# Attention and filter kernel: the seams between its stages laid over each other, with constant multiplies on PE in one wait

## The chip, the cores and the metric

The kernel runs as one program on one core of one Trainium2 chip. The metric is the device time of one execution in microseconds (us). A core has five engines with instruction streams of their own, which are ordered against each other by semaphores alone: PE (TensorE, matrix multiplies), DVE (VectorE), ACT (ScalarE), POOL (GpSimd) and SP (SyncE, which here issues every DMA). PE's clock has two levels, 1.2 and 2.4 GHz; the profile gives it as a share of the full one.

## The reference, cut to what matters

The input is x with shape (8, 512, 128, 128) in float32. Two layers are added to it in turn, each behind a group normalisation over 16 channels:

```python
def _gn(v, G=32, eps=1e-5):
    g = v.reshape(B_, G, C_ // G, H_, W_)
    m = jnp.mean(g, axis=(2, 3, 4), keepdims=True)
    s = jnp.var(g, axis=(2, 3, 4), keepdims=True)
    return ((g - m) / jnp.sqrt(s + eps)).reshape(v.shape)

# layer 0: 8 heads of 64 channels, S = H * W positions
A = jnp.einsum('mi,bhis->bhms', Wa, xh) + ba[:, None]
Bm = jnp.einsum('ni,bhis->bhns', Wb, xh) + bb[:, None]
V = jnp.einsum('ni,bhis->bhns', Wv, xh) + bv[:, None]
attn_maps = jax.nn.softmax(Bm, axis=-1)
attn_vecs = jax.nn.softmax(V, axis=2)
G = jnp.einsum('bhms,bhns->bhmn', A, attn_maps)
Z = jnp.einsum('bhmn,bhns->bhms', G, attn_vecs)

# layer 1: 12-tap separable filters; up by 2, bias, leaky, clip, down by 2
y = _upfirdn2d_sep(x, up_filter, UP, 1, PADDING, float(UP * UP))
y = y + bias[None, :, None, None]
y = jnp.where(y >= 0, y, y * SLOPE) * GAIN
y = jnp.clip(y, -CLAMP, CLAMP)
y = _upfirdn2d_sep(y, down_filter, 1, DOWN, (0, 0, 0, 0), 1.0)

x = x + layer0(_gn(x)); x = x + layer1(_gn(x))
```

## The kernel before, in words

The work is cut into 32 units of 128 channels of one image (two heads, eight normalisation groups). One pass of a loop, written out for each engine, does one unit. x is held twice: `xc` with channels on the partitions, `xh` with image rows on the partitions.

1. **Scores** (L1049 on PE, `max_b` L770 on DVE, `exp_b` on ACT, `gather_h` L439 on POOL): 32 blocks of four columns. ACT gathers a block of xc into `xcb`, a ring of four that lies in `yb` (L147), and PE projects it. DVE keeps a running maximum, ACT takes the exponential, PE transposes it, DVE copies that, and PE multiplies it with a block of xh that POOL has gathered into `xn`. POOL's gather waits until all of the unit's xh is loaded.
2. **Values** (L1087 on PE, `max_v` L818 on DVE): 32 blocks. Each block is projected twice, its maximum spread by POOL and subtracted by PE, the exponential taken and multiplied (`z`); DVE normalises it, POOL adds it to xh (L447).
3. **Norm 1, group 0** (L834 to L848): DVE takes the statistics of 16 channels of xh, PE averages them over the partitions (L1102), and the scales follow. Then batches 0 and 1 are normalised (L885, L891), in a high and a low float16 part (`xn_2`).
4. **Filters** (L1185 on PE, L604 on ACT, L928 on DVE, L484 on POOL): 16 batches g of eight images. In step i of batch g, PE makes the up-rows of image i of batch g+1 (`up_rows`, into bank 6), the up-columns of image i of g and the down-rows of image i-2. ACT evicts the up-rows (`t1` high) and the up-columns (`yb`), DVE makes the low part of t1 (L898) and the leaky step (L943), POOL clips (L458). In step 0, PE also makes the remainder rows from `t1r`, which POOL copies out of t1 (L487) as the first thing of a batch, after the clip of the batch before. Batch g+2 is normalised by ACT (L588, L592), and POOL makes its low part (L482). The statistics of group 1 are taken in step 0 of batch 0 (`group_stats`, L832).
5. **Tail** (L1220 on PE): what is left of batch 15, and between it norm 0 for the next unit: DVE's statistics and scales (L718 to L742), an average and a product on PE (L1006, L1010), a square root on ACT. The next unit's scores start when all of it is done.

The order on each engine is written out by hand. `steps` (L272) unrolls the first and last passes of a stage and loops over the ones between. `then_inc` raises a semaphore when an instruction ends, `wait_ge` holds the engine. On PE, the tail and the head of the unit are

```python
                for half in range(2):
                    down_remainder(half, last_ps[half])
...
                pe.wait_ge(s_y, IMG * NBAT * u + YCREDIT)
                pe.wait_ge(s_w, u + 1)
                proj_b(0, 0)
                proj_b(1, 1)
                pe.wait_ge(s_o, 2 * NBAT * u + OCREDIT)
                steps(pe, NBLK, RING, attend)
```

with the loop's jump between them.

## Time and profile before

| | |
|---|---|
| runs, us | 16610.16, 16631.77, 16636.97; median 16631.77 |
| profiled execution, us | 16617.44 (span 16615.7) |
| instructions in the span | 487793 |
| granted PE clock, mean | 0.96 |
| busy share of PE, DVE, ACT, POOL | 88%, 75%, 68%, 54% |
| DMA, mean | 72 GB/s |
| chain that ended last, by engine | PE 59%, DVE 14%, issue 8%, ACT 8%, POOL 5%, DMA 3% |
| DVE leaky step, 128x532 (L943), x4096 | mean 775 ns |
| POOL clip, 128x532 (L458), x4096 | mean 634 ns, idle before it 4108.1 us, ended by DVE L943 |
| PE, matmuls of the down rows (L987, dn_t with yb), x32768 | 4402.1 us busy |

The profile is that of one execution; its own time is 14 us under the median of the runs. The busy shares are means over stages that differ: in some stages PE has no gap, in others it mostly waits. "issue" is time in which an engine waited for nothing that the profile shows. All matmuls of a helper have one line (L987), so they are told apart by their tiles. Times in the trace are us from the start of the span. One unit takes 516.9 us (from 5226.7 to 5743.6 in the trace, the unit used below).

### The profile page before, as it was taken

Reading aid. Unit: us, or ns where it says so; the run is one execution under the profiler, and the core shown is the slowest. Engines: PE = TensorE matmul, PEld = TensorE weight load, DVE = VectorE, ACT = ScalarE, POOL = GpSimd, SP = SyncE. Lnnn points to the kernel's source line nnn. Section 1 sums busy time; section 2 is a strip of 40 time slices with the busy share of each in tenths; the row PEclk is TensorE's granted clock in tenths of the full one; section 3 lists DMA queues with packets and bytes.
Section 4 is the critical chain, followed back from the end, with each engine's and each line's share of the span. In section 5 each row is a group of like instructions: output and inputs, shape, how many; then the busy total and the mean of one; then the engine's idle time right before and its main releaser. Section 6 shows DMA issues by size and latency. Waiting matters only on the chain.

```text
span 16615.7 us, 487793 instructions
## 1 busy us (share of the span) xinstructions
PE 14628.5 (88%) x156388; PEld 12544.6 (75%) x156388; DVE 12382.1 (75%) x26154; ACT 11322.1 (68%) x19746; POOL 9035.6 (54%) x13589
## 2 busy tenths in 40 slices
PE   7898888988889888898888888888888889888898
PEld 5777777777777777777777777777777777777787
DVE  6777777777777777777777777777777777777776
ACT  5676666766667666676666666666667666676676
POOL 4555555555555555555555555555555555555555
PEclk9999999999999999999999999999999999999999
DMA  3233222332222332223322233222332223322232
GB/s 82 59 81 90 72 61 60 78 90 75 62 62 75 88 79 60 62 73 88 83 61 61 69 88 85 63 59 66 88 86 62 61 64 87 89 64 60 63 86 49
DMA packets 1931549, 1199.83 MB, mean 72 GB/s; under 512 B 78724, under 2 KB 1864580, under 8 KB 1930244
## 3 DMA queue, kind: packets, MB, share of 16 engines
q1 hardware_dynamic: 1930244, 1183.65, 27.6%
q8 instruction: 670, 10.98, 0.3%
q14 instruction: 635, 5.20, 0.1%
HBM read 537.30 MB, written 268.44 MB: 48 GB/s over the span
## 4 chain that ended last, share of the span: by engine, by line
PE 59%; DVE 14%; issue 8%; ACT 8%; POOL 5%; DMA 3%; DVEq 1%; POOLq 1%; SPq 1%; ACTq 0%
PE ps L987 57%; ACT yb L613 4%; DVE yb L943 4%; DVE xh L913 3%; POOL yb L458 3%; PE ps L1057 2%; ACT z L597 2%; DVE t L898 1%; DVE sth L832 1%; DMA out<-xh 1%; POOL t1r L487 1%; DVE z L904 1%; DVE stc L656 1%; DMA p<-t 1%; DMA xh<-in_x 1%
## 5 line engine op out<-in xcount | busy, mean ns | idle before, releaser
L458 POOL TENSOR_SCALAR yb<-yb 128x532 f32<-128x532 f32 x4096 | 2595.8, 634 | 4108.1 <-DVE yb L943 4108.1
L987 PE MATMUL ps<-dn_t,yb 128*128 128x64 f32 (+1 forms) x32768 | 4402.1, 278 | 10.5 <-POOL yb L458 10.5
L987 PEld LDWEIGHTS ps<-dn_t,yb 128*128 128x128 f32 x32768 | 4075.4, 196 | 19.7 <-POOL yb L458 14.4
L943 DVE SCALAR_TENSOR_TENSOR yb<-yb 128x532 f32<-128x532 f32 x4096 | 3174.6, 775 | 971.1 <-ACT yb L613 949.2
L613 ACT ACTIVATE yb<-ps,bias_b 128x532 f32<-128x532 f32 x4096 | 2881.2, 703 | 884.9 <-PE ps L987 794.9
L987 PE MATMUL ps<-up,xn 128*128 128x266 f16 x12288 | 2133.7, 287 | 640.0 <-DVE t L898 371.2
L585 ACT ACTIVATE t<-ps 128x266 f16<-128x266 f32 x4096 | 1587.6, 388 | 1534.5 <-PE ps L987 1482.0
L898 DVE TENSOR_TENSOR t<-ps,t 128x266 f16<-128x266 f32 x4096 | 1735.5, 426 | 801.2 <-ACT t L585 695.0
L987 PE MATMUL ps<-up_a,t 128*128 128x138 f16 x15360 | 2049.3, 225 | 11.2 <-DMA t<-p 11.0
L441 POOL COPY xn<-xh 128x512 f32 x1024 | 1090.6, 1067 | 1775.8 <-PE ps L987 1075.2
L987 PE MATMUL ps<-up_b,t 128*128 128x138 f16 x15360 | 2045.1, 224 | 0.0
L450 POOL TENSOR_TENSOR xh<-xh,pt 128x512 f32 (+1 forms) x1024 | 1692.0, 1652 | 524.2 <-DVE pt L815 521.1
L597 ACT ACTIVATE z<-ps 128x512 f16<-128x512 f32 x2048 | 1222.8, 597 | 721.3 <-PE ps L987 716.9
L987 PEld LDWEIGHTS ps<-up,xn 128*128 128x128 f16 x12288 | 1019.9, 103 | 872.9 <-DVE t L898 445.4
L904 DVE TENSOR_TENSOR z<-ps,z 128x512 f16<-128x512 f32 x2048 | 1405.4, 686 | 275.0 <-ACT z L597 205.9
L987 PEld LDWEIGHTS ps<-xn,pt 128*128 128x128 f32 x8192 | 1080.6, 194 | 559.0 <-issue 557.0
L987 PEld LDWEIGHTS ps<-gaug,p 128*128 128x128 f32 x8192 | 1070.1, 191 | 516.1 <-DVE pt L815 240.7
L987 PEld LDWEIGHTS ps<-up_a,t 128*128 128x128 f16 x15360 | 1347.2, 98 | 148.7 <-DMA t<-p 15.6
L482 POOL TENSOR_TENSOR xn<-xn 128x256 f16<-128x256 f32 x1792 | 1406.3, 805 | 0.0
L987 PEld LDWEIGHTS ps<-up_b,t 128*128 128x128 f16 x15360 | 1235.1, 98 | 0.0
L987 PE MATMUL ps<-yb,wbs 128*128 128x512 f32 x2048 | 1143.3, 649 | 99.8 <-ACT yb L533 95.8
L555 ACT ACTIVATE yb<-xc,sc 128x512 f32 (+1 forms) x1024 | 1198.5, 1170 | 0.0
(151 smaller groups left out, 27187.9 us busy)
## 6 DMA issues: line engine op xcount, KB each, us to landing
xc<-in_x SPq DMA_DIRECT2D x512, 512.0 KB, 3.8
xh<-in_x SPq DMA_DIRECT2D x480, 512.0 KB, 5.0
out<-xh SPq DMA_DIRECT2D x480, 512.0 KB, 3.4
p<-t SPq DMA_DIRECT2D x960, 128.0 KB, 3.0
t<-t SPq DMA_DIRECT2D x960, 128.0 KB, 2.4
t<-p SPq DMA_DIRECT2D x960, 128.0 KB, 2.4
xh<-in_x SPq DMA_DIRECT2D x64, 256.0 KB, 2.9
out<-xh SPq DMA_DIRECT2D x64, 256.0 KB, 3.0
```

What stands on the lines that cost most here:

```text
L441: nc.gpsimd.tensor_copy(xhb[par], xh_wc[:, bass.ts(k, WB), :]).then_inc(s_xhb, 1)
L450: nc.gpsimd.tensor_tensor(xv, xv, zs_[par][:].rearrange("p w h m -> p w (h m)"), ALU.add).then_inc(s_x1, 1)
L458: nc.gpsimd.tensor_scalar(v, v, CLAMP, -CLAMP, ALU.min, ALU.max).then_inc(s_yc, 1)
L482: return nc.gpsimd.tensor_tensor(xn_2[:, par, 1, c, :], xn[:, c, :], xn_2[:, par, 0, c, :], ALU.subtract)
L555: act.activation(xcb[r].rearrange("p (w h) -> p w h", w=WB), xc_wh[:, bass.ts(k, WB), :], ACT.Identity, bias=nm0).then_inc(s_xv, 1)
L585: act.activation(t1[:, par, 0, i, :], ps[:, bank, 0:UP], ACT.Copy).then_inc(s_th, 1)
L597: act.activation(z1[:, p // 2, 0, p % 2 * 2:p % 2 * 2 + 2, :, :].rearrange("p r c h -> p (r c h)"), dz_ps[p % 2], ACT.Copy).then_inc(s_zh, 1)
L613: act.activation(yb[:, i % YRING, :, :], y_ps[i % 2], ACT.Identity, scale=UPGAIN * GAIN, bias=bias_b[:, bass.ds(c0 + i, 1)]).then_inc(s_y, 1)
L898: nc.vector.tensor_tensor(t1[:, par, 1, i, :], ps[:, bank, 0:UP], t1[:, par, 0, i, :], ALU.subtract).then_inc(s_t1, 1)
L904: nc.vector.tensor_tensor(lo, dz_ps[p % 2], hi, ALU.subtract).then_inc(s_z1, 1)
L943: nc.vector.scalar_tensor_tensor(v, v, SLOPE, v, ALU.mult, ALU.max).then_inc(s_lr, 1)
L987: return nc.tensor.matmul(o, l, r, start=start, stop=stop, skip_group_check=share)
```

## The change

- **Scores of the next unit start in the tail.** `xcb` moves from yb into t1's half 0, free in the last batch. The last batch contains ACT's first four gathers, norm 0's steps on DVE, ACT and PE. In the tail the first four score blocks (`attend_first`, `exp_first`, `max_first`) stand between the last down rows and columns. The loop over score blocks starts at block 4. The tail's banks change (`last_ps`, `zr_ps`). The last unit is written out behind the loop on PE and ACT as well.
- **The last 16 channels of xh are loaded twice**: a copy for POOL's gather goes into xn_2 in the last batch (`load_copy`, 2 x 512 KB), and each gather becomes two copies.
- **Statistics of groups 0 and 1 under the values**: `block_stats`, two of 64 numbers per partition for each block.
- **PE multiplies constants** into bank 7: 42 times ahead of the wait for group 0's statistics and 26 times behind the average.
- **Batch 0 and 1**: normalisation in halves of four images; batch 1's on POOL (`first_batches`); in step 0 of batch 0, up-columns, eviction and leaky step come first.
- **All batches**: ACT's normalisation and POOL's low part in halves over four steps; `t1r` is copied ahead of the clip of image 7 of the batch before.

```diff
-        xcb = [yb[:, i, :, :].rearrange("p c u -> p (c u)")[:, 0:BS] for i in range(YRING)]
+        xcb_all = t1[:, 0, :, :, :].rearrange("p t i u -> p (t i u)").bitcast(fp32)
+        xcb = [xcb_all[:, i * BS:(i + 1) * BS] for i in range(RING)]
+        xlate = xn_2[:, :, :, :, :].rearrange("p a t i w -> p (a t i w)").bitcast(fp32).rearrange("p (c w) -> p c w", w=W)
+        xlate_wc = xlate.rearrange("p c w -> p w c")
...
+            def load_copy(u):
+                for i in range(0, LATE, IMG):
+                    sp.dma_start(xlate[:, i:i + IMG, :], x_row[u, :, P - LATE + i:P - LATE + i + IMG, :]).then_inc(s_xa, 16)
...
-                nc.gpsimd.tensor_copy(xhb[par], xh_wc[:, bass.ts(k, WB), :]).then_inc(s_xhb, 1)
+                nc.gpsimd.tensor_copy(xhb[par][:, :, 0:P - LATE], xh_wc[:, bass.ts(k, WB), 0:P - LATE])
+                nc.gpsimd.tensor_copy(xhb[par][:, :, P - LATE:P], xlate_wc[:, bass.ts(k, WB), :]).then_inc(s_xhb, 1)
...
+            def first_batches(u):
+                g = NBAT * u + 1
+                wait_alone(pool, s_r1, GROUPS * u + 1)
+                wait_alone(pool, s_xn, 2 * g)
+                for h in range(2):
+                    c = slice(h * HALF, (h + 1) * HALF)
+                    nc.gpsimd.tensor_scalar(xn[:, c, :], xh[:, IMG + h * HALF:IMG + (h + 1) * HALF, :], nm1[:, 0, 0:1],
+                                            r1[:, 0:1], ALU.add, ALU.mult).then_inc(s_xs, 1)
+                for h in range(2):
+                    norm_low_half(g, 1, h)
+                keep_rows(NBAT * u, 0)
...
             def clip_batch(u, j, par, before, after):
                 g = NBAT * u + j
-                wait_alone(pool, s_t1, IMG * (g + 1))
-                nc.gpsimd.tensor_copy(t1r[:, par, :, :, :], t1[:, par, :, :, 2 * P:UP].rearrange("p t i q -> p t q i")).then_inc(s_tq, 1)
                 for i in range(IMG):
+                    if i == IMG - 1 and after(1):
+                        keep_rows(g + 1, 1 - par)
                     clip_image(g, i, par)
                     if i == 1:
                         remainder_high(g, par)
                     if i == 2:
                         remainder_low(g, par)
                     now = 4 if before(1) else 6
-                    if after(2) and i in (now, now + 1):
-                        if i == now:
-                            wait_alone(pool, s_xnh, g + 3)
-                            wait_alone(pool, s_xs, g + 3)
-                        norm_low(par, 2 * (i - now))
-                        last = norm_low(par, 2 * (i - now) + 1)
-                        if i > now:
+                    if after(2) and i >= now:
+                        h, q = divmod(i - now, 2) if before(1) else (i - now, 0)
+                        if q == 0:
+                            wait_alone(pool, s_xnh, 2 * (g + 2) + h + 1)
+                            wait_alone(pool, s_xs, 2 * (g + 2) + h + 1)
+                        last = norm_low(par, 2 * h + q)
+                        if not before(1):
+                            last = norm_low(par, 2 * h + 1)
+                        if q or not before(1):
                             last.then_inc(s_xn, 1)
...
+                        now = 4 if first else LAG
+                        if i == now and after(2) and par == 0:
+                            act.wait_ge(s_r1, GROUPS * u + j // 2 + 2)
+                        if now <= i < now + 4 and after(2):
+                            if (i - now) % 2:
+                                xn_high(j + 2, par, 1, (i - now) // 2)
+                            else:
+                                norm(j + 2, 1, (i - now) // 2)
+                        if not after(1) and more:
+                            if i % 2:
+                                gather_first(u + 1, i // 2)
+                            if i == 4:
+                                sqrt0(u + 1)
...
+                if more:
+                    for k in range(RING):
+                        exp_first(u + 1, k)
...
+                def block_stats(k):
+                    for gr, st in enumerate((stc, stg)):
+                        last = nc.vector.bn_stats(st[:, bass.ds(k, 1), :].rearrange("p a b -> p (a b)"),
+                                                  xh[:, gr * GROUP:(gr + 1) * GROUP, bass.ts(k, WB)])
+                    return last
...
+                    if before(4):
+                        block_stats(k - 4)
...
-                        if first and i == 0:
-                            for p in range(4):
-                                last = group_stats(1, 1, p)
-                            last.then_inc(s_st1, 1)
...
+                        if more and not after(1):
+                            tail = base + N_SMALL - N_NORM0
+                            if i == 2:
+                                norm0_stats(u + 1, tail)
+                            if i == 4:
+                                norm0_variance(u + 1, tail)
+                            if i == 6:
+                                norm0_scales(u + 1, tail)
...
+                if more:
+                    max_first(u + 1, 0)
+                down_low(g, 3)
+                remainder_low(g, zr_ps)
+                if more:
+                    max_first(u + 1, 1)
                 for half in range(2):
-                    add_out(NBAT * (u + 1) - 1, NBAT - 1, half, last_ps[half])
+                    add_out(g, NBAT - 1, half, last_ps[half])
+                if more:
+                    for k in range(2, RING):
+                        max_first(u + 1, k)
...
+            def keep_busy(n):
+                for _ in range(n):
+                    mm(ps[:, 7, 0:UP], up_2[:, 0, 0:P], up_2[:, 0, :], True)
...
+                keep_busy(42)
                 pe.wait_ge(s_gn1, GROUPS * u + 1)
                 mm(tiny[:, 0:2], avg_p[:], mvh[:, 0, :], True).then_inc(s_gn1p, 1)
+                keep_busy(26)
...
+                        if not after(1) and more:
+                            if i == 3:
+                                norm0_average(u + 1)
+                            if i == 5:
+                                norm0_bias(u + 1)
...
                 steps(pe, NBAT, 2, batch, 2)
                 g = NBAT * (u + 1) - 1
+                if more:
+                    pe.wait_ge(s_w, u + 2)
+                    pe.wait_ge(s_y, IMG * (g + 1) - 1 + YCREDIT)
+                    proj_b(u + 1, 0, 0)
                 pe.wait_ge(s_z1, 4 * g + 2 + DCREDIT)
                 pe.wait_ge(s_o, 2 * g + OCREDIT)
                 down_columns(0, last_ps[0])
-                for i in range(IMG - LAG, IMG):
-                    if i == IMG - 1:
-                        norm0_average(u + 1)
-                    down_rows(g, i, 1)
+                down_rows(g, IMG - 2, 1)
+                if more:
+                    proj_b(u + 1, 1, 1)
+                down_rows(g, IMG - 1, 1)
                 pe.wait_ge(s_y, IMG * (g + 1) + YCREDIT)
+                pe.wait_ge(s_z1, 4 * g + 3 + DCREDIT)
                 remainder_columns(g, 1, zr_ps)
-                norm0_bias(u + 1)
+                if more:
+                    attend_first(u + 1, 0)
                 pe.wait_ge(s_z1, 4 * g + 4 + DCREDIT)
                 down_columns(1, last_ps[1])
                 pe.wait_ge(s_zr, g + 1 + ONE)
                 for half in range(2):
                     down_remainder(half, last_ps[half])
+                if more:
+                    pe.wait_ge(s_o, 2 * g + 1 + OCREDIT)
+                    attend_first(u + 1, 1)
+                    attend_first(u + 1, 2)
+                    pe.wait_ge(s_o, 2 * g + 2 + OCREDIT)
+                    attend_first(u + 1, 3)
```

POOL, steps 6 and 7 of a batch in the loop over batches, and the start of the next. L482 and L501 make the low part of xn, L487 and L512 the copy t1r, L458 and L477 the clip. Before:

```order
L482 TENSOR_TENSOR xn<-xn 128x256 x2
L269 REGISTER_ALU
L458 TENSOR_SCALAR yb<-yb 128x532
L269 REGISTER_ALU
L458 TENSOR_SCALAR yb<-yb 128x532
L461 COPY yc<-yb 128x2x20
L277 UNCONDITIONAL_BRANCH
L277 ISA
L487 COPY t1r<-t 128x160
L269 ISA
L458 TENSOR_SCALAR yb<-yb 128x532
```

With the change:

```order
L477 TENSOR_SCALAR yb<-yb 128x532
L275 REGISTER_ALU
L501 TENSOR_TENSOR xn<-xn 128x256
L275 REGISTER_ALU
L512 COPY t1r<-t 128x160
L275 REGISTER_ALU
L477 TENSOR_SCALAR yb<-yb 128x532
L480 COPY yc<-yb 128x2x20
L501 TENSOR_TENSOR xn<-xn 128x256
L283 UNCONDITIONAL_BRANCH
L283 ISA
```

The copy t1r stood behind the last clip and the jump of the loop; it stands ahead of the clip of image 7 now, and a quarter of the low part stands in each step.

PE, the end of a unit and the start of the next. wbs is the scaled weight of the scores, p0 and p1 the exponentials, xn the gathered block of xh. Before:

```order
L987 MATMUL ps<-dr_2,zr 128x4x5 x6
L1241 REGISTER_ALU
L1241 COMPARE_AND_BRANCH
...
L987 MATMUL ps<-yb,wbs 128x512
L1017 REGISTER_ALU
L987 MATMUL ps<-yb,wbs 128x512
L1066 REGISTER_ALU
L987 MATMUL ps<-yb,wbs 128x512
L1057 MATMUL ps<-ident,p0 128x128 x4
```

With the change:

```order
L1148 MATMUL ps<-ident,p1 128x128 x4
L1129 REGISTER_ALU
L1096 MATMUL ps<-t1,wbs 128x512
L1096 MATMUL ps<-xn,pt0 128x128 x4
L1148 MATMUL ps<-ident,p0 128x128 x4
L1366 REGISTER_ALU
L1129 REGISTER_ALU
L1096 MATMUL ps<-t1,wbs 128x512
L1096 MATMUL ps<-xn,pt1 128x128 x4
L1148 MATMUL ps<-ident,p1 128x128 x4
L1378 REGISTER_ALU
L1378 COMPARE_AND_BRANCH
```

The jump (COMPARE_AND_BRANCH) stood ahead of projection 0; it stands behind the transposes of block 3 now.

PE, from the last value block (gaug with p1) to the first row matmuls of batch 0 (up_2 with xn_2). Before:

```order
L987 MATMUL ps<-nident,tspr1 128x128 x4
L1081 REGISTER_ALU
L987 MATMUL ps<-gaug,p1 128x130 x4
L1101 ISA
L987 MATMUL ps<-mvh,avg_p 128x2
L1106 ISA
L987 MATMUL ps<-up_2,xn_2 128x266 x24
L1218 REGISTER_ALU
L1189 REGISTER_ALU
```

With the change:

```order
L1096 MATMUL ps<-nident,tspr1 128x128 x4
L1191 REGISTER_ALU
L1096 MATMUL ps<-gaug,p1 128x130 x4
L1096 MATMUL ps<-up_2 128x266 x42
L1212 ISA
L1096 MATMUL ps<-mvh,avg_p 128x2
L1096 MATMUL ps<-up_2 128x266 x26
L1218 ISA
L1096 MATMUL ps<-up_2,xn_2 128x266 x12
L1218 REGISTER_ALU
L1096 MATMUL ps<-up_2,xn_2 128x266 x12
```

Constants (up_2 with up_2) stand on both sides of the average, and the rows come in two halves, each behind a wait of its own.

## Rows read from the trace of the kernel before

**Rows 1.** The page's table of engines: busy us (share of span) x instructions.
```profile
PE 14628.5 (88%) x156388; PEld 12544.6 (75%) x156388; DVE 12382.1 (75%) x26154; ACT 11322.1 (68%) x19746; POOL 9035.6 (54%) x13589
```

**Rows 2.** Windows: us, PE, PEld, DVE, ACT, POOL busy, PE clock, DMA share, GB/s.
```profile
5325.00:5400.00 75.00, 75.00 (x535) 51.98 (x534) 41.86 (x84) 61.86 (x83) 61.98 (x57) 1.00 0.04 14
...
5444.00:5464.00 20.00, 16.06 (x194) 14.92 (x194) 12.13 (x24) 10.88 (x20) 10.03 (x19) 0.83 0.25 61
...
5483.50:5523.00 39.50, 35.55 (x484) 33.49 (x482) 32.86 (x65) 27.21 (x49) 22.94 (x43) 1.00 0.47 121
```

**Rows 3.** Timeline of PE, seam A: start us, length us, operation, idle before and its releaser.
```profile
5224.66 0.90 PE L987 MATMUL ps<-dn,z 128*128 128x64 f16 x24
...
5237.32 5.21 PE L987 MATMUL ps<-yb,wbs 128*128 128x512 f32 x6 [3.38 <-ACT yb L533]
...
5248.35 1.51 PE L987 MATMUL ps<-xn,pt 128*128 128x128 f32 x8 [3.23 <-POOL xn L441]
...
5253.62 1.02 PE L987 MATMUL ps<-yb,wbs 128*128 128x512 f32 x2
...
5255.81 1.02 PE L987 MATMUL ps<-yb,wbs 128*128 128x512 f32 x2
```

**Rows 4.** Timeline of all engines, seam A: DVE, ACT and POOL.
```profile
5232.33 0.15 DVE L733 RECIPROCAL sc<-sc 128x1 f32<-128x1 f32 x1
...
5234.16 0.17 DVE L741 MEMSET mrun<- 128x128 f32 x1
...
5234.89 3.98 ACT L533 ACTIVATE yb<-xc 128x512 f32<-128x512 f32 x4 [2.75 <-issue]
...
5238.89 1.28 ACT L545 ACT_TABLE_LOAD   x1
...
5247.15 2.06 POOL L441 COPY xn<-xh 128x512 f32 x2 [20.29 <-DMA xh<-in_x]
```

**Rows 5.** Timelines, seams B and C, and DVE's long aggregate (5226.91).
```profile
5226.91 1.02 DVE L720 BATCH_NORM_AGGREGATE mvc<-stc 128x2 f32<-128x192 f32 x1
...
5404.24 1.16 PE L987 MATMUL ps<-gaug,p 128*128 128x130 f32 x8 [0.85 <-DVE pt L815]
...
5408.41 2.47 DVE L832 BATCH_NORM_STATS2 sth<-xh 128x6 f32<-128x512 f32 x4 [1.97 <-POOL xh L450]
...
5411.89 0.59 PE L987 MATMUL ps<-mvh,avg_p 128*128 128x2 f32 x2 [6.49 <-DVE mvh L838]
...
5415.63 1.23 DVE L891 TENSOR_TENSOR xn<-xn 128x1024 f16<-128x1024 f32 x1 [0.40 <-ACT xn L592]
...
5416.91 4.20 PE L987 MATMUL ps<-up,xn 128*128 128x266 f16 x24 [4.44 <-DVE xn L891]
...
5429.41 0.38 PE L987 MATMUL ps<-mvh,avg_p 128*128 128x2 f32 x2 [4.59 <-DVE mvh L858]
...
5448.36 0.85 PE L987 MATMUL ps<-up,xn 128*128 128x266 f16 x3 [3.48 <-POOL xn L482]
```

**Rows 6.** Groups by line: count, busy us, mean ns, idle us before and its releasers.
```profile
L987 PE MATMUL ps<-up,xn 128*128 128x266 f16 x12288 | 2133.7, 287 | 640.0 <-DVE t L898 371.2 <-DVE xn L891 142.0 <-POOL xn L482 111.3
...
L656 DVE BATCH_NORM_STATS2 stc<-xc (+1 forms) x1024 | 695.9, 682 | 0.0
```

**Rows 7.** The tile t1r on PE: what ended the idle time before it, us, times.
```profile
  POOL t1r L487: 348.8, 438
```

**Rows 8.** Timeline of all engines at the start of a batch.
```profile
5491.22 0.42 DVE L898 TENSOR_TENSOR t<-ps,t 128x266 f16<-128x266 f32 x1
...
5491.77 0.51 PE L987 MATMUL ps<-up,t1r 128*80 128x266 f16 x3 [0.68 <-POOL t1r L487]
...
5492.11 0.50 PE L987 MATMUL ps<-up,xn 128*128 128x266 f16 x3
```

**Rows 9.** Timeline of DVE: a leaky step that runs beside POOL's subtraction.
```profile
5484.51 1.21 DVE L943 SCALAR_TENSOR_TENSOR yb<-yb 128x532 f32<-128x532 f32 x1
```

357 lines of the change are left out of this document (200 added, 157 removed).

## The prediction

> **What bounds the kernel now.** I read the engine table first: PE is busy for 88% of the span and no other engine for more than 75% [rows 1]. That is a mean over stages, so I cut one unit of work (of 32) out of the trace, from 5226.7 to 5743.6 us, 516.9 us long. In the value blocks PE has no gaps (75.00 busy of 75 us, which are 28 blocks of 2.68 [rows 2]); nothing that is done for the other engines there can bring time. In the filter batches PE is busy for 35.55 of 39.50 us [rows 2]; one cause of its gaps comes back in nearly every batch, the wait for POOL's copy of the remainder rows [rows 7]. The rest lies at the seams, where a chain of short steps over three engines runs with PE idle, and where PE's granted clock is down at its 1.2 GHz level when it resumes: between filters and next scores [rows 3, 4], between values and filters, in batch 0 and ahead of batch 1 [rows 5]. The seams together hold some 50 us of each unit in which PE does much less than it could.
>
> **Seam A: last batch to next scores (31 times).** From PE's last column work inside the last batch (5224.66) to the first step of the loop over score blocks (5253.62) pass 29.0 us [rows 3]. In it: norm 0's statistics and scales, PE at the slow clock (six projections took 5.21 us, two at full clock 1.02), a jump back to the unit's start, and 3.23 us of waiting for POOL, which had itself waited 20.29 us for the last loads of xh [rows 3, 4]. The work of PE in this stretch at full clock: four score steps at 2.19 (5253.62 to 5255.81 [rows 3]), 8.8, and about 4.1 of down rows and columns: 12.9 us. With the change I lay the chain out from 5224.66:
> - The scaled weights. The chain of small DVE steps (about 2.0 us from the reciprocal to the memset of mrun [rows 4]) now stands after image 6 of the last batch. ACT gets four gathers of about 1.0 us (3.98 for four [rows 4]), a table load of 1.28 and a wait for the variance in that batch; I push image 6 by 1.1 for it. Weights ready: 5227.9, so PE idles 3.2 us.
> - Then projection 0, down columns, down rows, projection 1, down rows, remainder and projection 2 back to back, 5.8: 5233.7. ACT must do two evictions, the table load (1.28 [rows 4]) and the exponential (about 0.9) behind the remainder: PE transposes block 0 at 5235.6.
> - Down columns, then add_out behind DVE's copy of the transposes; steps 1 to 3 with one maximum, copy and exponential each: ends at 5243.6.
> - The jump to the unit's start now stands between step 3 and the loop, with nothing over it. PE paid 3.38 us there before (before 5237.32; ACT's first gather, begun at 5234.89 and 1.0 long, explains only a part) and ACT 2.75 [rows 3, 4]. I take 3.2: 5246.8.
>
> That is 6.8 us less than 5253.62. Against it stands the clock: this layout has idle stretches of 3.2, 1.9 and 3.2 us, and before, the clock fell inside this seam after shorter ones. If a third of the 12.9 us of work runs at half clock, about 4 are lost. I take a gain of 3 us (bounds: 0, with nearly all of it slow and the gathers in PE's way, and 7, with none slow): 31 x 3 = 93.
>
> The Trainium skill (Runtime: NRT & Kernel Launch, section Instruction fetch mechanics) says that a taken branch to code outside the small fetched window stalls the engine until it is fetched from memory. By that rule the jump is not made cheaper by having more work ready; the 2.75 us of ACT with nothing to wait for agree with it [rows 4]. Without the jump the gain would be 10 us at full clock.
>
> **Seam B: values to filters (32 times).** Before, DVE takes the four group-0 statistics (2.47 us) when the last value block has been added, and PE averages at 5411.89 [rows 5]. Now two short statistics per block are taken under the values; behind the last add stand one pair (about 0.4) and an aggregate over 192 numbers, 1.02 us long [rows 5]. The average comes at 5410.5, 1.4 us sooner. The last value block ends at 5405.4 [rows 5]; PE's 42 multiplies go on to 5410.2 at 0.113 each (a group of three is 0.34 long, 5491.77 to 5492.11 [rows 8]), so they end just before it; the 26 end 2.9 after the average, near 5413.8. From average to first rows it was 5.0 us before; halves of DVE's two and of ACT's one operation (the subtraction alone took 1.23 [rows 5]) save about 1.5, so the first half of the normalised rows is ready at about 5414.0. So the constants cost nothing, and the 24 first row matmuls, which took 4.20 from 5416.91 [rows 5], run 5414.0 to 5416.8 with the second half's wait in them: 4.3 sooner. Batch 1's normalisation moves to POOL (two at about 0.6, four at 0.65 to 0.8), and the remainder copy stands behind it: that costs about 1.3 us of PE's wait. Group 1's four statistics on DVE go from batch 0, which shortens the wait of 4.59 before the average at 5429.41 [rows 5]; it becomes 3.4 because the aggregate is the long form. I get 5424.9 for that average: gain 4.5 (bounds 2 and 6.5), 32 x 4.5 = 144.
>
> **Seam C: ahead of batch 1 (32 times).** PE waits 3.48 us for the normalised rows of batch 2 [rows 5] and comes out slow. The clock's mean of 0.83 over 20 us [rows 2] is about 6.8 us at the lower level, some 5 of them work, so 2.4 us lost. The change halves the normalisation on ACT and POOL and starts it one image earlier; the first half is due just when PE asks. Of 5.9 I take 5.4 (bounds 2.5 and 5.9): 32 x 5.4 = 173.
>
> **D: the wait in each batch.** PE waited 348.8 us in all for t1r, 438 times [rows 7], 0.80 each. The copy now stands ahead of POOL's clip of image 7; it needs the low part of image 7 only, which DVE makes before the leaky step that the clip waits for, so POOL does it in a gap. But PE's next step needs DVE's low part of image 0: in the batch shown that ends at 5491.64, while PE would be there at 5491.43. The row matmuls that started at 5492.11 start at about 5491.72: gain 0.39 [rows 8]; the same in the next batch gives 0.67. Mean 0.53 x 438 = 232 (bounds: 100 and 349). DVE and ACT wait for PE several times in each batch, so they follow when PE is sooner.
>
> **What costs nothing.** The gather of xh as two POOL copies (about 1.3 where one took half of 2.06 [rows 4]) fits in a score step of 2.19. The two extra loads of 512 KB per unit run in the last batch, where the DMA engines have room, and only POOL's gather waits for them. The statistics under the values: DVE is busy 41.86 of 75 us there, 1.5 a block [rows 2], so it idles 1.2; the 512-wide form takes 0.68 [rows 6], and a 64-wide one I put at 0.2, nearer to the smallest steps (0.15 [rows 4]); the bounds are these two. Two per block fit; at 0.68 each they would overrun by 0.2 a block.
>
> **Sum.** 93 + 144 + 173 + 232 = 642 us, off the profiled execution's 16617.4: 15975. The median of the runs is 14 us above that execution, so 15990 us.
>
> **Rivals.**
> 1. The batch wait only changes its name: DVE, saturated over images 5 to 7, takes D back. For it: PE already waits for DVE's low parts in those batches (371.2 us in all [rows 6]). Against: DVE idles before and after. Time: 15990 + 232 = 16220.
> 2. The clock: PE comes to the constants slow or falls in seam A altogether. 68 matmuls at 0.225 instead of 0.113 end 7.6 us later, which eats B; and A becomes a loss of 3. Then only C and D remain, less 93: 16632 - 405 + 93 = 16320. For it: the clock fell in seam A after short gaps. Against: PE is at full clock when it enters the constants.
> 3. Slower: DVE's statistics under the values hold up POOL. They read xh, as POOL's add does; POOL is busy 61.98 of 75 us there, 2.21 a block [rows 2]. If POOL could not work during them and each took 0.68, a block's 2.68 would become 2.21 + 1.36 + 0.35 for semaphores = 3.92, and 30 blocks x 32 units x 1.24 = 1190: 17180. It decides from a hold-up of about 1.1 us a block. For it: DVE's leaky step, 0.775 in the mean (the table of the profile), took 1.21 where POOL's subtraction ran beside it [rows 9]. Against: the statistics of xc keep a mean of 0.682 wherever they fall [rows 6].
> 4. More than forecast: A at 7 and D at 349: 15990 - 124 - 117 = 15750.
> 5. The gains and losses cancel within 0.2%, 16632: no mechanism speaks for it.
>
> The Trainium skill (SBUF — State Buffer, section Who interferes with whom) lets a DVE instruction with one SBUF input run beside GpSimd and makes one with two SBUF inputs exclude a GpSimd read. By it the leaky step collides and the statistics don't, and rival 3 is void; the rows of xc agree, but none shows statistics beside the add.
>
> **Chances.** Forecast 0.58, rival 1 0.16, rival 2 0.11, rival 3 0.05, rival 4 0.07, rival 5 0.03. A measurement of this kernel can tell about 0.2% (33 us) from no change. Faster: 0.58 + 0.16 + 0.11 + 0.07 = 0.92; same 0.03; slower 0.05. The range leaves out rivals 3 and 5 and the ends of 2 and 4: 15740 to 16330.
>
> **What would show it.** A: the loop of score blocks starts 22 to 29 us after the last column work instead of 29.0, and an idle stretch near 3 us stands before it with nothing to wait for. B: the clock stays at 2.4 GHz to the first row matmuls, which start 8.6 us after the last value block (11.5 before). C: no wait on POOL's xn at batch 1. D: t1r no longer ends a PE wait, and the period of two batches falls from 39.4 to about 38.3. Wrong would be: value blocks longer than 2.68, a last batch over 19 us, or t1r's wait turned into one for DVE's t of equal size.

## The result, and the profile after

The changed kernel takes 16027 us (median of 4 runs, 16020.7 to 16040.8) against 16634 us for the kernel before on the same chip: ratio 0.9639, 95% interval 0.9622 to 0.9656. The forecast was 15990 us in a range of 15740 to 16330. The profiled executions span 16615.7 and 16039.0 us, 577 us apart (the medians are 607 apart); the rows below are read against each other. One execution of the kernel with the early weights, further below, took 25629 us at a mean granted clock of 0.58 where its five others took 15804 to 15813, and is in no median.

The engine table after, beside [rows 1]:

```profile
PE 14771.9 (92%) x158560; PEld 12616.3 (79%) x158560; DVE 12345.0 (77%) x27932; ACT 11570.1 (72%) x20705; POOL 9299.4 (58%) x14805
```

To see where the 577 us went I cut every unit at named matmuls of PE and took the mean over units 2 to 31 (start to start, us; "low" is how much of the stretch stood at the low granted clock, 1.2 GHz):

| stretch of a unit | before | low | after | low | change |
|---|---|---|---|---|---|
| score loop and value blocks | 150.62 | 0.0 | 152.09 | 3.3 | +1.47 |
| last value block to group-1 average (B) | 25.82 | 13.2 | 21.79 | 1.1 | -4.03 |
| group-1 average to batch 2's start (C) | 40.79 | 11.3 | 35.01 | 3.5 | -5.78 |
| batches 2 to 14 (D) | 254.18 | 0.0 | 247.13 | 0.0 | -7.05 |
| last batch, to its last column work | 11.86 | 0.0 | 11.37 | 0.0 | -0.49 |
| from there to the score loop (A) | 33.37 | 16.6 | 31.90 | 14.4 | -1.47 |

The sum is 17.35 us a unit, 555 in 32 units; the other 22 lie at the ends, most of them in the last unit. The last batch's 0.49 us belongs to D: PE's wait for t1r there, 0.70 us a unit before, is gone. The windows after answer to [rows 2]: a steady stretch of value blocks, the stretch behind group 1's average, and two steady batches, which now take 38.15 us instead of 39.4:

```profile
5150.00:5225.00 75.00, 75.00 (x533) 51.93 (x532) 48.51 (x139) 62.11 (x83) 61.60 (x57) 1.00 0.04 14
5250.00:5270.00 20.00, 17.14 (x156) 15.33 (x157) 14.30 (x30) 12.72 (x24) 10.09 (x19) 0.91 0.16 35
5305.06:5343.21 38.15, 35.39 (x481) 33.11 (x479) 31.80 (x64) 28.18 (x53) 22.65 (x43) 1.00 0.50 128
```

DVE's busy time under the value blocks went from 41.86 to 48.51 of 75 us, and PE's stayed at 75.00: the statistics are there and cost nothing.

PE's timeline over seams B and C, beside [rows 5] (start, length, operation, idle time before and its releaser):

```profile
5229.48 1.16 PE L1096 MATMUL ps<-gaug,p 128*128 128x130 f32 x8 [0.85 <-DVE pt L898]
5230.47 4.92 PE L1096 MATMUL ps<-up 128*128 128x266 f16 x42
5235.61 0.38 PE L1096 MATMUL ps<-mvh,avg_p 128*128 128x2 f32 x2 [0.22 <-DVE mvh L932]
5235.85 3.11 PE L1096 MATMUL ps<-up 128*128 128x266 f16 x26
5239.47 2.91 PE L1096 MATMUL ps<-up,xn 128*128 128x266 f16 x24 [0.51 <-DVE xn L988]
...
5245.95 0.51 PE L1096 MATMUL ps<-up,t1r 128*80 128x266 f16 x3 [1.39 <-POOL t1r L512]
...
5250.83 0.38 PE L1096 MATMUL ps<-mvh,avg_p 128*128 128x2 f32 x2 [3.35 <-DVE mvh L953]
...
5267.03 0.52 PE L1096 MATMUL ps<-up,xn 128*128 128x266 f16 x3 [1.25 <-POOL xn L501]
```

The 24 first row matmuls take 2.91 us instead of 4.20, and batch 1's first rows wait 1.25 us for POOL instead of 3.48. In the batches the wait for the remainder rows is gone but for batch 0, and DVE's took back 81 of the 304 us; these are the lists of what PE waited for, total us, times, longest, beside [rows 6, 7]:

```profile
PE ps L1096 <- DVE t L995: 452.4, 948, 1.0
...
PE ps L1096 <- issue: 73.5, 30, 3.2
...
PE ps L1096 <- POOL t1r L512: 44.4, 32, 1.5
```

Seam A comes in two kinds. Of its 30 passages in units 2 to 31, 17 take 33.6 to 34.2 us, 9 take 28.5 to 29.1, and 4 lie between. First a long one, then a short one, on PE, beside [rows 3]:

```profile
5042.93 0.92 PE L1096 MATMUL ps<-dn,z 128*128 128x64 f16 x24 [0.39 <-DVE xh L1010]
...
5051.87 2.07 PE L1096 MATMUL ps<-t,wbs 128*128 128x512 f32 x2 [3.08 <-DVEq L817]
5053.73 1.55 PE L1096 MATMUL ps<-dn,z 128*128 128x64 f16 x24
5055.09 1.96 PE L1096 MATMUL ps<-dn_t,yb 128*128 128x64 f32 x8
5056.84 2.01 PE L1096 MATMUL ps<-t,wbs 128*128 128x512 f32 x2
...
5074.66 0.60 PE L1148 MATMUL ps<-ident,p 128*128 128x128 f32 x4
5077.33 1.30 PE L1096 MATMUL ps<-t,wbs 128*128 128x512 f32 x2 [2.07 <-issue]
```

```profile
3054.49 2.07 PE L1096 MATMUL ps<-t,wbs 128*128 128x512 f32 x2 [3.07 <-DVEq L817]
3056.36 1.40 PE L1096 MATMUL ps<-dn,z 128*128 128x64 f16 x24
3057.59 1.08 PE L1096 MATMUL ps<-dn_t,yb 128*128 128x64 f32 x8
3058.51 1.07 PE L1096 MATMUL ps<-t,wbs 128*128 128x512 f32 x2
...
3071.35 0.60 PE L1148 MATMUL ps<-ident,p 128*128 128x128 f32 x4
3074.94 2.07 PE L1096 MATMUL ps<-t,wbs 128*128 128x512 f32 x2 [2.99 <-issue]
```

Both wait 3.1 us for the scaled weights, and both come out at the low clock (2.07 us for a projection of 1.02). In the short one the clock is back after the column work, 3.4 us after it fell; in the long one the same down rows take 1.96 instead of 1.08, and so on for 20.5 us, though PE is busy for most of them. The three passages of 30.2 to 30.6 us have 10.2 us of low clock. The windows of the two, with the granted clock behind the busy times (0.69 and 0.93):

```profile
5043.85:5077.33 33.48, 26.83 (x191) 19.95 (x188) 16.35 (x41) 14.96 (x27) 7.69 (x14) 0.69 0.24 69
3046.47:3074.94 28.47, 19.89 (x192) 15.27 (x188) 16.10 (x40) 14.77 (x27) 7.70 (x14) 0.93 0.29 82
```

### The profile page after: what moved, and what is told of

Its sections match the earlier page's. It is cut to its first block, busy times and chain, and to the rows that moved or that the text cites. A ratio compares the mean times of both kernels' runs of the same rounds, so it can differ in the third digit from the quotient of the medians.

```text
span 16039.0 us, 502759 instructions
## 1 busy us (share of the span) xinstructions
PE 14771.9 (92%) x158560; PEld 12616.3 (79%) x158560; DVE 12345.0 (77%) x27932; ACT 11570.1 (72%) x20705; POOL 9299.4 (58%) x14805
## 4 chain that ended last, share of the span: by engine, by line
PE 50%; DVE 23%; issue 12%; ACT 8%; POOL 5%; DVEq 2%; POOLq 0%; SPq 0%; DMA 0%; ACTq 0%
PE ps L1096 49%; ACT z L653 5%; DVE xh L1010 3%; DVE nblk L836 3%; DVE yb L1039 2%; DVE t L995 2%; DVE stc L731 2%; DVE nrun L840 1%; DVE mrun L825 1%; DVE srun L824 1%; POOL yb L477 1%; POOL xb L493 1%; DVE z L1001 1%; DVE bexp L843 1%; ACT alpha L590 1%
## 5 line engine op out<-in xcount | busy, mean ns | idle before, releaser
L477 POOL TENSOR_SCALAR yb<-yb 128x532 f32<-128x532 f32 x4096 | 2588.0, 632 | 3789.9 <-DVE yb L1039 3784.3
L1039 DVE SCALAR_TENSOR_TENSOR yb<-yb 128x532 f32<-128x532 f32 x4096 | 3041.7, 743 | 831.1 <-ACT yb L670 820.4
L1096 PE MATMUL ps<-up,xn 128*128 128x266 f16 x12288 | 2057.7, 278 | 518.0 <-DVE t L995 452.4
L459 POOL COPY xn<-xh 128x448 f32 x1024 | 981.2, 958 | 1544.4 <-PE ps L1096 1364.1
L1096 PEld LDWEIGHTS ps<-up,xn 128*128 128x128 f16 x12288 | 948.1, 100 | 814.5 <-DVE t L995 608.8
L1096 PE MATMUL ps<-t,wbs 128*128 128x512 f32 x2048 | 1179.8, 661 | 196.8 <-DVEq L817 99.1
L501 POOL TENSOR_TENSOR xn<-xn 128x256 f16<-128x256 f32 x1920 | 1331.9, 697 | 1.8
L608 ACT ACTIVATE t<-xc,sc 128x512 f32 (+1 forms) x1024 | 1198.4, 1170 | 0.0
```

The source lines that it names most:

```text
L459: nc.gpsimd.tensor_copy(xhb[par][:, :, 0:P - LATE], xh_wc[:, bass.ts(k, WB), 0:P - LATE])
L477: nc.gpsimd.tensor_scalar(v, v, CLAMP, -CLAMP, ALU.min, ALU.max).then_inc(s_yc, 1)
L501: return nc.gpsimd.tensor_tensor(xn_2[:, par, 1, c, :], xn[:, c, :], xn_2[:, par, 0, c, :], ALU.subtract)
L608: act.activation(xcb[r].rearrange("p (w h) -> p w h", w=WB), xc_wh[:, bass.ts(k, WB), :], ACT.Identity, bias=nm0).then_inc(s_xv, 1)
L1039: nc.vector.scalar_tensor_tensor(v, v, SLOPE, v, ALU.mult, ALU.max).then_inc(s_lr, 1)
L1096: return nc.tensor.matmul(o, l, r, start=start, stop=stop, skip_group_check=share)
```

## The experiments

My theory after these rows: B, C and D went as forecast; seam A lost its gain to the low clock, which PE's idle wait for the weights lets in, and to the jump to the unit's start. Rivals: the seam is bound by the chain over DVE and ACT; the wait in the batches is only renamed; the statistics or the constants cost something. Each number below is the median of 5 runs unless said otherwise, with the ratio to the kernel before and its interval; the changed kernel has 0.9639 (0.9622 to 0.9656). The runs come from several chips, on which the kernel before took 16614 to 16634 us, so a difference of some 20 us between two medians says nothing by itself; the ratios are the safer comparison. No run takes the halved normalisation (in B and C) out by itself.

### Seam A: hold the clock

```diff
-                    pe.wait_ge(s_w, u + 2)
                     pe.wait_ge(s_y, IMG * (g + 1) - 1 + YCREDIT)
+                    keep_busy(26, 0)        # constants into bank 0
+                    pe.wait_ge(s_w, u + 2)
```

> The changed kernel plus 26 multiplications of constants (2.9 us at the high clock) where PE waits 3.1 us for the scaled weights in seam A. In the changed kernel's trace the 31 seams (from the last column matmul inside the last batch to the loop over score blocks; 33.4 us before the change) fall in two groups: 12 of 28.5 to 30.6 us, 19 of 33.6 to 34.2, the long ones with some 20 us at the low granted clock; mean 31.9. Theory (the idle wait for the weights lets the clock fall, and that ate seam A's gain): the first projection takes 1.0 instead of 2.07 us, all 31 seams take 27 to 29 us, 31 x 3 to 4.5 = 95 to 140 us less than the changed kernel: 15890 to 15930 us. Rival 1 (the clock falls for the later short waits and the jump just the same): the long seams stay, 16000 to 16030 us. Rival 2 (the seam is bound by the chain over DVE and ACT, not by PE's speed): under 20 us gained, though the clock is high.

15903 us, ratio 0.9567 (0.9554 to 0.9580). All 30 passages are under 29 us (mean 28.17, low clock 3.8 instead of 14.4 us). PE in one of them:

```profile
5012.95 3.11 PE L1096 MATMUL ps<-up 128*128 128x266 f16 x26
5016.04 1.12 PE L1096 MATMUL ps<-t,wbs 128*128 128x512 f32 x2
...
5023.84 0.66 PE L1148 MATMUL ps<-ident,p 128*128 128x128 f32 x4 [1.73 <-ACT p L592]
```

The projection takes 1.12 us and the wait stays as long as it was, filled; behind it PE still waits 1.73 us for ACT's exponential. 124 us for holding the clock in one wait of 3 us: the theory holds, and both rivals fall.

### Seam A: the weights sooner

```diff
+            def norm0_weights(n, done):        # reciprocal and wbs only
+                ...
+                dve.sem_inc(s_w, 1)
...
+                        if more and not after(1) and i == 5:
+                            norm0_weights(u + 1, base + N_SMALL - N_NORM0)
                         dve.wait_ge(s_y, IMG * g + i + 1 + YCREDIT)
```

PE waits for these weights alone before projection 0, and for the other scales only before it transposes block 0.

> The changed kernel with the scaled score weights made one image earlier in the last batch: DVE's reciprocal and the scaling of wb stand ahead of the leaky step of image 5 instead of behind that of image 6, and PE waits for them alone before projection 0 (for the rest of the scales before the transposes of block 0). No constants are added. Theory (PE's wait of 3.1 us for the weights is both a loss by itself and what lets the clock fall for some 20 us in 19 of 31 seams): the wait goes, the long seams of 33.8 us vanish, and the mean seam falls from 31.9 to 25 to 26.5 us, 31 x 5.4 to 6.9 = 170 to 215 us: 15810 to 15860 us, below the 15903 of the kernel with constants in that wait. Rival 1 (the chain over image 7's clip, ACT's table load and the first exponential is what ends last, so PE only waits later): about the same as with constants, 15890 to 15920 us. Rival 2 (DVE's leaky step, pushed back by 1 us, delays the last down rows by as much): 15940 us or more.

15804 us, ratio 0.9514 (0.9501 to 0.9527): as the theory has it, 6 us under its range. A further run of the same program gave the profile:

> The same program as the one with the early weights (15804 us), for a profile of an execution at the usual clock. Theory: PE doesn't wait for the weights, seams of 25 to 26.5 us without a long stretch at the low clock, and the standstill at the jump of 2 to 3 us still there. Rival: the gain came from elsewhere, and the wait stands behind projection 0 (for the rest of the scales or for the first exponential) with seams of 28 us.

15805 us (one run). PE in one seam:

```profile
4978.92 0.92 PE L1102 MATMUL ps<-dn,z 128*128 128x64 f16 x24 [0.39 <-DVE xh L1014]
...
4983.81 1.11 PE L1102 MATMUL ps<-dn_t,yb 128*128 128x64 f32 x8 [0.26 <-POOL yb L477]
...
4984.92 1.10 PE L1102 MATMUL ps<-t,wbs 128*128 128x512 f32 x2
...
4992.69 0.66 PE L1154 MATMUL ps<-ident,p 128*128 128x128 f32 x4 [1.73 <-ACT p L592]
```

No wait for the weights, no long passage; the mean seam is 24.92 us, 7.0 less than in the changed kernel, and its first projection starts 5.3 us instead of 8.2 us after the last column work. The price, DVE's leaky step pushed back, shows as a wait of 0.26 us.

### Seam A: the jump

The boundary of the loop over units is put where PE, ACT and DVE wait anyway (each unit's code is cut in two parts, part 1 being the seam):

```diff
+            with eng.Fori(0, UNITS - 2) as u:
+                unit(u, True, 1)
+                unit(u + 1, True, 0)
```

> The changed kernel with the boundary of the loop over units moved: PE, ACT and DVE now jump back where each of them waits anyway in seam A (PE before the wait for the scaled weights, 3.1 us; ACT before the last down rows' eviction, 7.6 to 10 us; DVE behind the first block's maximum, 3.4 us) and not between score blocks 3 and 4, where PE stood still for 2.1 to 3.0 us with nothing to wait for and came out at the low clock. Theory (the jump itself costs 2 to 3 us, and is hidden under a wait of that length): PE runs from block 3 into block 4 without a gap, 30 x 2.0 to 4.0 = 60 to 120 us less than the changed kernel: 15910 to 15970 us. Rival 1 (the standstill belongs to that place, as one engine's wait for another, and not to the jump): it stays, 16020 to 16035 us. Rival 2 (the jump adds to the wait for the weights instead of lying under it): the gap only moves, 16010 to 16040 us.

15995 us, ratio 0.9626 (0.9613 to 0.9639), 32 us less than the changed kernel by the medians and 21 by the ratios, whose intervals overlap: not the 60 to 120 of the theory, and hardly more than nothing. In the profiled executions a unit is 1.5 us shorter. PE at the old place of the jump and at the new one:

```profile
5039.86 2.07 PE L1113 MATMUL ps<-t,wbs 128*128 128x512 f32 x2 [2.98 <-DVEq L829]
...
5061.30 1.02 PE L1113 MATMUL ps<-t,wbs 128*128 128x512 f32 x2
...
5063.49 1.02 PE L1113 MATMUL ps<-t,wbs 128*128 128x512 f32 x2
```

The two projections at the old place follow each other in 2.19 us, PE's waits with nothing to wait for fall from 73.5 us in 30 to 22.3 in 27, and the score loop with the value blocks takes 150.67 us again, so the standstill went with the jump and is mostly hidden. But 21 of 30 passages are now over 31.5 us (17 in the changed kernel), with 17.4 us a unit at the low clock (14.4 there): most of what the jump gave, the clock took. So a second form: fewer jumps, with the clock held.

```diff
+            unit(0, True)
+            with pe.Fori(0, (UNITS - 2) // 5) as k:
+                for i in range(5):
+                    unit(5 * k + (i + 1), True)
```

> The changed kernel with the 26 constants in the wait for the weights, and the loop over units written out five times per pass on PE, ACT and DVE: 6 jumps back to the start in place of 31, and 25 of the 31 seams run straight on into the loop over score blocks. Theory (the jump costs PE 2 to 3 us of standing still, and the low clock behind it 1.4 us more): 25 x 3.4 to 4.4 = 85 to 110 us less than the 15903 us of the kernel with constants: 15790 to 15820 us. Rival 1 (the standstill is not the jump's but that of new code, reached for the first time in a unit): it stays in all seams, 15890 to 15915 us. Rival 2 (a longer program makes each engine wait for code in many places): slower than 15920 us.

15837 us, ratio 0.9533 (0.9520 to 0.9546), 66 us below the kernel with the constants alone. PE's waits with nothing to wait for fall from 72.3 us in 30 to this:

```profile
PE ps L1100 <- DMA t<-p: 12.4, 12, 2.4
PE ps L1100 <- issue: 12.0, 5, 3.3
```

Of the 30 jumps that the changed kernel takes back to the start 5 are left, and the standstill with them: it is that of the jump, not of new code. The seam and the stretch behind it fell by 3.5 us a unit as expected, and the rest of the unit lost 1.9. A part of that is in the first line: PE waits for the DMAs that swap t1's halves, which it never did in the changed kernel. These 12.4 us are 0.4 a unit; what took the remaining 1.5 is open.

### D alone, and D undone

```diff
+                if before(1):
+                    keep_rows(g, par)
                 for i in range(IMG):
-                    if i == IMG - 1 and after(1):
-                        keep_rows(g + 1, 1 - par)
                     clip_image(g, i, par)
```

> The changed kernel with POOL's copy of the remainder rows put back to the start of each batch (the term D of the forecast, 232 us, undone). Theory (D as forecast): PE waits for t1r in nearly every batch again, about 0.8 us, and the time goes up by 200 to 260 us, to 16230 to 16290 us. Rival (the wait only changed its name, since PE waits for DVE's low part of the rows anyway; its total went from 371 to 452 us): up by 0 to 60 us, under 16090 us.

16839 us (6 runs, two of them 16723 and 16755, four from 16839 to 16851; the profile is of the one of 16755), ratio 1.0134 (1.0118 to 1.0149): 812 us slower than the changed kernel, and slower than the kernel before. Neither theory nor rival had that. PE waits for t1r in every batch; these are all engines at one start of a batch:

```profile
PE ps L1096 <- POOL t1r L512: 847.6, 512, 2.1
```

```profile
5587.77 0.67 POOL L501 TENSOR_TENSOR xn<-xn 128x256 f16<-128x256 f32 x1
...
5588.19 0.81 DVE L1039 SCALAR_TENSOR_TENSOR yb<-yb 128x532 f32<-128x532 f32 x1
5588.38 0.95 POOL L512 COPY t1r<-t 128x160 f16<-128x160 f16 x1
...
5589.47 0.51 PE L1096 MATMUL ps<-up,t1r 128*80 128x266 f16 x3 [1.75 <-POOL t1r L512]
```

The halved normalisation (part C) gives POOL a subtraction behind image 7. In the mean over the batches but the first, the copy starts 3.0 us after DVE's low part of image 7 (2.5 in the kernel before) and takes 0.90 us (0.46 before), and PE's wait grows from 0.73 to 1.67 us by the sum of the two. The copy is longer because DVE's leaky step has begun ahead of it. It is as long in the changed kernel (median 0.95 us), where PE doesn't wait for it. So the early copy pays for what C would cost in the batches; that C is the cause is read from this order on POOL, and no run undoes C alone. The other half of the pair, the early copy in the kernel before:

```diff
-                wait_alone(pool, s_t1, IMG * (g + 1))
-                nc.gpsimd.tensor_copy(t1r[:, par, ...
                 for i in range(IMG):
+                    if i == IMG - 1 and after(1):
+                        keep_rows(g + 1, 1 - par)
                     clip_image(g, i, par)
```

> The kernel before with one part of the change alone: POOL's copy of the remainder rows (t1r) of the next batch ahead of the clip of image 7. Theory of the forecast (the copy is 0.8 us late in each batch, 348.8 us in all, and PE's next wait takes a part of it back): 100 to 349 us faster than before, near 230. What the last run with the copy put back showed (812 us slower than the changed kernel, 1.66 us of wait in each batch) says that it was not the same wait there: the halved normalisation keeps POOL busy to the end of a batch. So, if that holds, this run gives the part of D that stands by itself, 16280 to 16530 us. Rival (in the old order POOL's copy ahead of the clip delays the clip, and down rows wait instead): 16600 us or slower.

16501 us, ratio 0.9933 (0.9919 to 0.9946): 113 us. PE's wait for t1r is gone (348.8 to 0), DVE's went from 371.2 up:

```profile
PE ps L992 <- DVE t L903: 516.9, 943, 1.0
```

So alone, D gives back 146 of 349 us to DVE's t; batches 2 to 14 take 249.4 us instead of 254.2 (154 us in 32 units), and the seams lose a part again. D's worth is 113 by itself and 812 on top of the rest of the change.

### The constants

```diff
-                keep_busy(42)
                 pe.wait_ge(s_gn1, GROUPS * u + 1)
                 mm(tiny[:, 0:2], avg_p[:], mvh[:, 0, :], True).then_inc(s_gn1p, 1)
-                keep_busy(26)
```

> The changed kernel without the 42 and 26 multiplications of constants in seam B. Theory (the constants cost no time and hold the clock): PE enters the first row matmuls at the low clock and stays there through batch 0, as before the change, where 24.5 us of each unit between the last value block and batch 2 were at the low clock; at half to two thirds of that as work, 4 to 8 us more per unit: 32 x 4 to 8 = 130 to 260 us over the changed kernel, 16160 to 16290 us. Rival 1 (batch 0 is bound by ACT, DVE and POOL, and PE's clock matters little there): at most 1.5 us per unit, 16030 to 16080 us. Rival 2 (the constants delay the average or the first rows): faster than the changed kernel, under 16010 us.

16174 us, ratio 0.9731 (0.9717 to 0.9744), 147 us over the changed kernel. That is in the theory's range, but only half of it for the theory's reason. Of 4.2 us a unit, 2.1 lie between group 0's average and batch 2, where 4.7 us stood at the low clock and now 15.5 do. The other half is nowhere near: in scattered batches PE waits for the swapping DMAs (35.0 us, 1.1 a unit), and 3.5 us of each unit in batches 2 to 15 stand at the low clock, where none did.

```profile
PE ps L1096 <- DMA t<-p: 35.0, 37, 2.3
```

The same in the kernel before, with 56 and 37 constants:

> The kernel before with another part of the change alone: PE multiplies constants while it waits between values and filters, 56 ahead of the group average and 37 behind it (the old waits of 6.49 and 4.44 us are longer than the new ones). Theory (the clock's fall is worth something by itself): the first row matmuls and batch 0 run at the high clock; without the constants the changed kernel lost 147 us, of which 66 were between the average and batch 2; here some 2 to 4 us per unit, 65 to 130 us faster than before: 16490 to 16560 us. Rival 1 (with the old order batch 0 is bound by the normalisation on ACT and POOL, and the speed of PE counts for nothing): 16590 to 16630 us. Rival 2 (the constants keep the average waiting): slower than 16640 us.

16587 us (11 runs), ratio 0.9983 (0.9974 to 0.9992): 27 us less than before, 0.9 a unit, and just under rival 1's range. The rows run at the high clock (2.91 us for the 24), and the time is then waited for further on:

```profile
5409.45 2.91 PE L987 MATMUL ps<-up,xn 128*128 128x266 f16 x24 [0.23 <-DVE xn L891]
5414.57 0.51 PE L987 MATMUL ps<-up,xn 128*128 128x266 f16 x3 [2.21 <-DVE t L898]
...
5421.83 0.58 PE L987 MATMUL ps<-mvh,avg_p 128*128 128x2 f32 x2 [4.59 <-DVE mvh L858]
```

Here the high clock was worth only what the chain beside PE let through. Then the constants in another wait, ahead of group 1's average:

```diff
+                            if first and i == 2:
+                                pe.wait_ge(s_yr, g + 1)
+                                keep_busy(26)
                             up_rows(g + 1, i, 1 - par, ...
```

> The changed kernel with 26 more multiplications of constants in batch 0, in PE's wait of 3.35 us for group 1's statistics. Behind that wait the trace shows 3.5 us at the low granted clock in each unit, between 5252.5 and 5255.9 us in the unit shown. Theory (the idle stretch lets the clock fall, and the work behind it takes twice its time): the low clock goes there, 1.0 to 1.7 us per unit, 30 to 55 us: 15975 to 16000 us. Rival (batch 0 ends with POOL's normalised rows, for which PE waits 1.25 us at batch 1 anyway; what PE gains it waits for there): 16015 to 16035 us.

15935 us, ratio 0.9588 (0.9575 to 0.9601), 92 us less than the changed kernel and under both ranges. Between this average and batch 1 the low clock is gone (3.5 us to 0), which is worth 0.4 us a unit there, less than expected. Most of the gain stands in seam A, where nothing was changed: 2 of 30 passages over 31.5 us instead of 17, mean 29.04.

### The statistics under the values

```diff
+                    for gr in range(2 if r is not None else 0):
+                        nc.vector.bn_stats(spare[:, r % 2, gr, :], xh[:, gr * GROUP:(gr + 1) * GROUP, bass.ts(k, WB)])
```

> The changed kernel with two more short statistics of the same data in 28 of the 32 value blocks (their results are not used), so four a block where the change has two; this doubles the cost that the forecast put at nothing. In the changed kernel's trace a short one takes 0.21 to 0.22 us and stands beside POOL's addition, and a block takes 2.68 us as before. Theory (DVE has the time, and statistics, which read one operand from SBUF, don't hold up POOL's addition, which reads the same tile): DVE's 0.25 us more per block lies in its idle time, the block stays at 2.68: 16010 to 16045 us. Rival (DVE's chain per block, or POOL behind it, is near its limit): up to 0.3 us per block, 28 x 32 x 0.3 = 270 us: 16100 to 16300 us.

15948 us, ratio 0.9592 (0.9579 to 0.9605): not the same time, but less. All engines but PE and ACT in one value block:

```profile
5152.02 0.34 DVE L904 BATCH_NORM_STATS2 spare<-xh 128x6 f32 x2
5152.27 0.21 DVE L906 BATCH_NORM_STATS2 stc<-xh  x1
5152.40 0.21 DVE L906 BATCH_NORM_STATS2 stg<-xh  x1
5152.43 1.65 POOL L470 TENSOR_TENSOR xh<-xh,pt 128x512 f32 x1 [0.55 <-DVE pt L899]
...
5155.04 1.64 POOL L470 TENSOR_TENSOR xh<-xh,pt 128x512 f32 x1 [0.41 <-DVE pt L899]
```

POOL's addition keeps its 1.65 us, and the score loop and value blocks take 152.3 us against 152.1 (3.7 and 3.3 us of it at the low clock). So doubled statistics cost at most 0.2 us a unit. The gain is again seam A's: 10 of 30 long passages instead of 17, mean 30.12. Nothing in the rows makes it a merit of the statistics. The profiled execution is the slowest of the five (15995 us, the others 15929 to 15951).

### All together

The early weights, the constants ahead of group 1's average and the loop written out five times:

> Three edits together on the changed kernel: the weights one image earlier (alone 15804 us), the 26 constants in the wait for group 1's statistics (they took the low clock out of batch 0, where it cost 0.4 to 0.6 us per unit), and the loop over units written out five times (25 of 31 jumps gone; with the constants in seam A that gave 66 us, 2.6 per jump). Theory (the three don't overlap, since each removes a stretch of its own): 15804 - 66 - 31 x 0.5 = 15722 us, between 15690 and 15745. Rival 1 (without the jump PE reaches the loop sooner and only waits for DVE's chain per block): 15770 to 15805 us. Rival 2 (the longer program moves the DMAs that swap t1's halves against the loads, as in some units of the written-out kernel, whose PE waits 12 times for them): 15750 to 15800 us.

15826 us, ratio 0.9517 (0.9504 to 0.9530): no faster than the early weights alone. Seam A fell to 23.28 us and the stretch behind it to 150.68, but PE waits for the swapping DMAs again, and in 23 of 28 cases in batches 2 to 15 the clock falls within 6 us of such a wait (6.1 us a unit at the low clock there, none in the changed kernel):

```profile
PE ps L1106 <- DMA t<-p: 52.4, 45, 2.7
```

That is rival 2 of the expectation, with its range missed on the upper side. The best version is the one with the early weights, 15804 us, 223 below the changed kernel.

## Why the prediction was right, point by point

- **Sum.** 642 us were forecast off the profiled execution and 577 measured. B 144 against 129 (4.03 a unit), C 173 against 185, D 232 against 241 (226 in batches 2 to 14, 15 in the last), and A 93 against nothing: the 1.47 us won up to the loop go again behind it. The miss of 93 stayed small beside the whole, and C and D gave back some 20 of it.
- **Seam A: the term that was mis-sized.** The step that failed is "if a third of the 12.9 us of work runs at half clock, about 4 are lost". The wait for the weights ahead of it was right, 3.08 us against 3.2. The trace has the lower bound of the forecast in it, 17 passages with 20.5 us at the low clock that gain nothing (33.8 against 33.4 us), and 9 short ones that gain 4.8 of the 7 of the upper one. The forecast took a mean state, the seam has two. The kernel with held clock shows the price, 124 us. The second loss was not in the layout at all: behind the jump the score loop now starts at the low clock (3.3 us of it a unit, none before).
- **Seam A: a wrong starting point.** I called the column work at 5224.66 [rows 3] the last inside the last batch. It is the first of the last batch's own; the last inside it starts at 5219.38. In the changed order projection 0 stands ahead of the piece I began with, so the forecast's 22 to 29 us and its 29.0 of before cannot be compared with anything after. From the true common point, the last column matmul of the group at 5219.38, it is 33.4 before and 28.5 to 34.2 after.
- **The jump.** Forecast 3.2 us with nothing to wait for; measured 1.8 to 3.2 in 30 seams, 73.5 us in all. That it costs this where PE's work is ready is shown: written out, 25 of 30 are gone. The Trainium skill (Runtime: NRT & Kernel Launch, section Instruction fetch mechanics) says that a taken branch to code outside the fetched window holds the engine until that code has come. These rows agree with it.
- **Seam B.** The average came 1.5 us sooner (1.4 forecast; constants 4.92 us, then 0.22 of wait). The first rows start 8.8 us after the last value block's end (8.6 forecast, 11.5 before), with the clock at the high level throughout, in all 30 units, as said. The wait for POOL's t1r, put at 1.3, is 1.39, and that for group 1's average, put at 3.4, is 3.35.
- **Seam C.** Gain 5.78 against 5.4. The wait was to go and is 1.25 us still, but PE comes out of it at the high clock, and batch 1 takes 18.65 us instead of 21.43. The other 3.0 us were won ahead of it, between the average and batch 1.
- **D.** 304 us of t1r's wait gone, 81 back as DVE's: 223 net against 232. The size was right as a part of this change. As a part by itself it was not: alone 113, and its removal costs 812. The sum of the forecast added the parts as if each stood by itself, and that its D fits is in part luck: it was worked out from waits in the order of the kernel before, where it is worth 113.
- **Rivals.** 1 (the wait only renamed) fell for the whole, with 81 of 304 us to its credit. 2 (the clock) came true in seam A and behind its jump, and nowhere else; PE entered the constants at the high clock. 3 (statistics hold up POOL) is refuted by doubling them; the Trainium skill (SBUF — State Buffer, section Who interferes with whom) says that a DVE instruction with one SBUF input, outside the two-port modes, doesn't contend with GpSimd, and that one with two contends with a GpSimd instruction that reads SBUF. The rows agree on both: the addition keeps 1.65 us, and POOL's copy takes 0.95 us where the leaky step, with both inputs in SBUF, has begun ahead of it.

## What to carry to other kernels

Fill or remove an idle wait of 3 us that stands ahead of dense PE work: here a wait of 3.1 us cost 7.2 per passage (223 us in 31), the wait itself and some 4 us through the clock (124 us in 31, what filling it gave), so removing it beat filling it. Before parts are added up, ask which part frees the resource that another one fills; here only the pair of experiments, one part alone and one part undone, told it. And before a gain is credited to an edit, look at the stretch of the trace that it touched.

## What the runs showed that I had not expected

- Seam A's passages are long or short with nothing in between but a few, and their share differs between kernels that differ only elsewhere in the unit: 17 of 30 over 31.5 us in the changed kernel, 10 with doubled statistics, 2 with constants in batch 0, 21 with the jump moved, 0 with the wait filled or gone. Each count is of one execution, and the executions of one kernel differ as well (15929 to 15995 us with doubled statistics, at mean clocks of 0.988 to 0.982), so a part of this may be chance. In the changed kernel the clock fell 6.7 to 7.6 us after the last column work in the long ones and 7.7 us or later in the short ones. What sets that moment stays open.
- The DMAs that swap t1's halves land late in some kernels only: PE waited for them 0 times in the changed kernel, 37 without constants (35.0 us), 12 and 45 in the written-out ones (12.4 and 52.4 us), 18 with the jump moved (7.7 us), and 17 in the kernel before (11.0 us). Why is open; no run here varied the loads that share the queue with them.
- Who begins first decides who pays where POOL's small copy meets DVE's leaky step. In the changed kernel the leaky step has begun in 415 of 512 cases, and the copy takes 0.95 us instead of 0.46. In the kernel before the copy begins first in 430 of 437 such meetings and keeps its 0.46 us; in the 153 of them where the leaky step starts less than 0.2 us behind it, that step takes 0.91 us instead of 0.71.
